# A cross-attention kernel: transposed context of the last two tiles from memory, weight scans spread over the tiles

## What is computed

```python
x1 = layernorm(x)                                # x2 = x1_2 = ctx_2048
energy = jnp.einsum('bcn,bmn->bcm', x1, x2)      # b=16, c=64, m=1601, n=1024
attn = jax.nn.softmax(energy, axis=-1)
attn = attn / (RENORM_EPS + attn.sum(axis=1, keepdims=True))
x_r = jnp.einsum('bcm,bmn->bcn', attn, x1_2)
t = x1 - (jnp.einsum('oc,bcn->bon', conv_w, x_r) + conv_b[None, :, None])
# batch norm over (b, n), relu, x = x + x1 + relu(...)
```

## Time and profile before

| | |
|---|---|
| median of 3 runs | 1379.93 us (1379.62 to 1380.21) |
| the profiled execution | 1379.24 us, span 1377.4 us |
| TensorE busy | 1334.1 us (97%) |
| VectorE busy | 878.7 us (64%) |
| ScalarE busy | 495.1 us (36%) |
| stage one ends (last `weigh_ctx`) | 484.8 us from the start |

### The profile page before, as it was taken

One profiled execution on the slowest core, in us unless ns is written; L12 is line 12 of the kernel. 1 busy time (PEld: TensorE's weight loads), 2 busy tenths in 40 slices (PEclk: granted clock), 3 DMA queues, 4 the chain that ended last, 5 costly groups with the idle time before them and its releaser, 6 DMA issues.

```text
span 1377.4 us, 17833 instructions
## 1 busy us (share of the span) xinstructions
PE 1334.1 (97%) x6850; PEld 651.2 (47%) x6850; DVE 878.7 (64%) x1484; ACT 495.1 (36%) x765; POOL 2.4 (0%) x10
## 2 busy tenths in 40 slices
PE   7999999999999979999999999999999999999994
PEld 4554646444454434444555555444444444444442
DVE  3232424324242288888889996755999997777974
ACT  1121302113021122116877775112545455544432
POOL 0000000000000000000000000000000000000000
PEclk9999999999999989999999999999999999999998
DMA  9999999999999587845565669341487775222264
GB/s 379 419 421 420 421 422 420 422 421 421 417 398 393 234 321 255 315 168 164 161 182 154 172 174 339 107 168 52 167 271 226 242 264 196 77 77 77 77 180 152
DMA packets 141044, 356.25 MB, mean 259 GB/s; under 512 B 63008, under 2 KB 89760, under 8 KB 115360
## 3 DMA queue, kind: packets, MB, share of 16 engines
q1 hardware_dynamic: 137792, 343.56, 68.5%
q10 hardware_dynamic: 3168, 11.54, 2.1%
HBM read 308.40 MB, written 46.66 MB: 258 GB/s over the span
## 4 chain that ended last, share of the span: by engine, by line
PE 74%; issue 14%; DMA 6%; DVE 4%; ACT 1%; DVEq 0%; POOLq 0%; POOL 0%
PE ps L1048 13%; PE ps L1153 13%; PE ps L1309 9%; PE ps L1220 8%; PE ps L962 7%; PE ps L1269 6%; PE ps L1107 5%; PE ps L1000 4%; DMA ctxT<-in_ctxT 3%; PE ps L979 2%; PE ps L1030 2%; PE ps L982 2%; DMA w_scan<-in_w2t 1%; PE ps L1173 1%; DMA x_t<-in_x 1%
## 5 line engine op out<-in xcount | busy, mean ns | idle before, releaser
L1358 PE MATMUL ps<-t_half,hl 128*128 128x512 f16 x896 | 193.6, 379 | 0.0
L1048 PE MATMUL ps<-ctx_sb,attnT 128*64 128x512 f32 (+1 forms) x832 | 180.3, 593 | 0.0
L699 ACT ACTIVATE stg<-ps 128x512 f32<-128x512 f32 (+1 forms) x80 | 44.4, 555 | 345.5 <-PE ps L979 173.4
L1358 PEld LDWEIGHTS ps<-t_half,hl 128*128 128x128 f16 x896 | 87.7, 98 | 105.7
L962 PE MATMUL ps<-ctxT,x1T 128*64 128x512 f32 x512 | 115.8, 596 | 1.8 <-DMA ctxT<-in_ctxT 1.8
L872 ACT ACTIVATE hl<-hb,al 128x512 f16<-128x512 f32 x112 | 79.2, 720 | 97.4 <-PE ps L1358 83.7
L1048 PEld LDWEIGHTS ps<-ctx_sb,attnT 128*64 128x64 f32 (+1 forms) x832 | 58.9, 137 | 115.4 <-issue 108.0
L1862 DVE SCALAR_TENSOR_TENSOR hl<-hb,al,hl 128x512 f16<-128x512 f32 x112 | 81.9, 749 | 48.7 <-ACT hl L872 48.5
L1107 PE MATMUL ps<-wv_sb,x2T 128*128 128x512 f32 x256 | 112.0, 596 | 0.0
L1220 PE MATMUL ps<-wo_sb,oT 128*128 128x512 f32 x256 | 111.6, 593 | 0.3 <-ACT oT L778 0.3
L1456 DVE COPY stg<-ps 128x512 f32<-128x512 f32 (+1 forms) x80 | 50.9, 639 | 82.2 <-PE ps L982 43.0
(11 more groups left out here) (220 smaller groups left out, 1810.5 us busy)
## 6 DMA issues: line engine op xcount, KB each, us to landing
ctxT<-in_ctxT SPq DMA_DIRECT2D x64, 1024.0 KB, 22.4
...
ctx_sb<-in_ctx SPq DMA_DIRECT2D x16, 2048.0 KB, 32.5
...
```

Of the source, the lines that this page charges most:

```text
L1048: ins = mm(bank(ea + hf)[C * b:C * b + C, :], attnT[0:w, slots[mt], C * b:C * b + C], ctx_sb[0:w, mt, b, hf * BANK:hf * BANK + BANK], star ...
L1358: ins = mm(bank(b), hl[:, r % RING, n, s * P:s * P + P], t_half[:, r % BRING, :], start=(fresh and k == 0 and n == 0), stop=(k == HK - 1 a ...
```

## The change

The host supplies two more arrays: `ctxW`, the transposed copy of the 512 wide rows (1 MB holds two of the 8 chunks), and `ctxE`, the transposed tail of the last tile (two parts of 0.27 MB). `LOADED` says how many of the eight wide chunks a tile takes from memory: none in tiles 0 to 5, four in tile 6, eight in tile 7, which also takes its tail from there. Tile 6 so has six pairs in place of ten, tile 7 none. Two of the 1 MB pieces go through the ring of `ctxT`, behind the tile's eight chunks; the other two of tile 7 go to `stg`, and its tail to the places of `x_t` and of a part of `x1T`, once tile 6's energies are done (`load_apart`). The last tile's groups of `ctx_sb` are loaded in the order in which `weigh_ctx` takes them. `tok` and `xo` are loaded in two parts each, and the second parts stand behind `wv_sb`. 40 scans in place of 48 stand in the value stage: 2 in tile 2, 6 in tile 3, 7 in each of tiles 4 to 7 and 4 behind, each tile's in three portions, one of them between the statistics and the square root's use. 24 in place of 16 stand in the projection stage, four ahead of `normal(H)` and four in each tile until they are done.

```diff
@@ -56,16 +56,40 @@
 U = len(UNITS)
 
 SINGLES = [(mt, half) for mt in range(TM, MT) for half in range(2)]
-PAIRS = [("wide", c) for c in range(NC)] + SINGLES[-2:]
-E = len(PAIRS)
-assert len(SINGLES) == E
+LOADED = (0,) * (NT - 2) + (4, NC)
+
+
+def pairs(p):
+
+    if p < BY_ROW:
+        return SINGLES
+    return [("wide", c) for c in range(LOADED[p], NC)] + (SINGLES[-2:] if p < NT - 1 else [])
+
+
+def first_pair(p):
+
+    return sum(len(pairs(q)) for q in range(p))
+
+
+def slots_of_tile(p):
+
+    ring = [(p, "chunk", c) for c in range(NC)] + [(p, "wide", i) for i in range(min(LOADED[p] // 2, 2))]
+    return ring if p < NT - 1 else ring + [(p, "apart", i) for i in range(2)]
+
+
+USES = [use for p in range(NT) for use in slots_of_tile(p)]
+USE_NO = {use: n for n, use in enumerate(USES)}
+RING_NO = {use: n for n, use in enumerate([use for use in USES if use[1] != "apart"])}
+RING_USES = list(RING_NO)
+
 H = 8
 D = 64
 HID = 4096
 HC = HID // P
 WT = HID * N // P // 1024
 WH = WT // H
-SCANS_V = 48
+SCANS_V = 40
+V_SCANS = (0, 0, 2, 6, 7, 7, 7, 7, 4)
 EPS = 1e-5
 LAMBDA_INIT = 0.8 - 0.6 * math.exp(-0.3 * 12)
...
@@ -382,6 +407,18 @@
 
         def width(mt):
             return P if mt < MT - 1 else TAIL
+
+        def slot(use):
+
+            return ctxT[:, RING_NO[use] % SLOTS, :, :] if use[1] != "apart" else stg[:, 2 * use[2]:2 * use[2] + 2, :, :]
+
+        def halves(use):
+
+            return slot(use) if use[1] == "apart" else slot(use).rearrange("p c (b m) -> p c b m", b=2)
+
+        def used_by(p):
+
+            return USE_NO[p, "chunk", NC - 1] + 1
...
-            def load_T(q, chunks):
+            def load_T(q, chunks, kind="chunk"):
                 for c in chunks:
-                    k = NC * q + c
+                    use = (q, kind, c)
+                    k = RING_NO[use]
                     if k >= SLOTS:
-                        sp.wait_ge(ctxT_used, k - SLOTS + 1)
-                    sp.dma_start(ctxT[:, k % SLOTS, :, :], ctxT_in[q, c]).then_inc(ctxT_got[k % SLOTS], 16)
+                        sp.wait_ge(ctxT_used, USE_NO[RING_USES[k - SLOTS]] + 1)
+                    to, src = (slot(use), ctxT_in[q, c]) if kind == "chunk" else (halves(use), ctxW_in[q, c])
+                    sp.dma_start(to, src).then_inc(ctxT_got[k % SLOTS], 16)
+
+            def load_apart():
+
+                sp.wait_ge(e_done, first_pair(NT - 1))
+                for i in range(2):
+                    sp.dma_start(slot((NT - 1, "apart", i)), ctxW_in[NT - 1, 2 + i]).then_inc(apart_got, 16)
+                for i in range(2):
+                    sp.dma_start(tails[i][:, :, :, :], ctxE_in[i]).then_inc(apart_got, 16)
...
                     load_T(p + 1, range(7, NC))
+                    load_T(p + 1, range(min(LOADED[p + 1] // 2, 2)), "wide")
+                    if p + 1 == NT - 1:
+                        load_apart()
+                        next_N((5, 7, 0, 1, 2, 6, 3, 4))
+                        break
                     next_N(range(0, 5))
                 if p == 0:
                     sp.dma_start(lam_sb[:, 0:4 * D], lambdas.partition_broadcast(P)).then_inc(lam_in, 16)
                 if p + 2 < NT:
-                    load_T(p + 2, range(0, 4 if p < 2 else 2))
+                    load_T(p + 2, range(0, 4 if p < 2 or LOADED[p + 1] else 2))
                 next_N(range(5, 6))
-                if p >= 2 and p + 2 < NT:
+                if p >= 2 and p + 2 < NT and not LOADED[p + 1]:
                     load_T(p + 2, range(2, 4))
                 next_N(range(6, G))
                 if p + 2 < NT:
                     load_T(p + 2, range(4, 6))
 
...
-            sp.wait_ge(ctxT_used, NC * NT)
+            def load_tok(t0, t1):
+                sp.dma_start(tok[:, t0:t1, :], n_dram[t0:t1].rearrange("t p n -> p t n")).then_inc(n_in, 16)
+
+            def load_xo(t0, t1, s):
+                sp.dma_start(xo[:, t0:t1, :], x_v[t0:t1].rearrange("t p n -> p t n")).then_inc(s, 16)
+
+            sp.wait_ge(ctxT_used, len(USES))
             sp.wait_ge(n_stored, 16 * (NT - 1))
-            sp.dma_start(tok[:, 0:NT - 1, :], n_dram[0:NT - 1].rearrange("t p n -> p t n")).then_inc(n_in, 16)
+            load_tok(0, 2)
             sp.wait_ge(pv_done, G * NT - 7)
-            for i in range(2):
-                h4 = slice(4 * i, 4 * i + 4)
-                sp.dma_start(xo[:, h4, :], x_v[h4].rearrange("t p n -> p t n")).then_inc(s_in[i], 16)
+            load_xo(0, 2, s_in[0])
             sp.wait_ge(pv_done, G * NT - 3)
             sp.dma_start(wv_sb[:, :, :], wv.rearrange("(c p) n -> p c n", p=P)).then_inc(wv_in, 16)
+            load_tok(2, NT - 1)
+            load_xo(2, NT, s_in[1])
             sp.wait_ge(pv_done, G * NT)
...
                     A(stg[:, e % 4, 0, 0:n], bank(pair_bank(p, e, 0), n), ACT.Copy).then_inc(act_tr_out, 1)
-                    if e == 2 and p + 1 < NT:
+                    if e == (2 if not LOADED[p] else 0) and p + 1 < NT:
                         sqrt(p + 2, slice(0, 1))
...
-                if t + 2 < NT:
+                if 1 <= t < NT - 2:
                     relu(t + 2)
...
                       ACT.Copy).then_inc(x2_out, 1)
+                if t == 0:
+                    act.wait_ge(n_in, 32)
+                    relu(2)
                 act.wait_ge(xs_ready, t + 1)
...
-                for g in [e // 2] if e % 2 == 0 and (p < BY_ROW or e == 8) else range(4) if e == 0 else []:
+                for g in [e // 2] if e % 2 == 0 and p < BY_ROW else range(4) if e == 0 else [4] if e == len(pairs(p)) - 2 else []:
...
+            def loaded_energies(p):
+
+                wides = [u for u in slots_of_tile(p) if u[1] != "chunk"]
+                for j, use in enumerate(wides):
+                    if use[1] == "apart":
+                        pe.wait_ge(apart_got, 64)
+                    else:
+                        k = RING_NO[use]
+                        pe.wait_ge(ctxT_got[k % SLOTS], 16 * (k // SLOTS) + 16)
+                    for i in range(2):
+                        c = 2 * j + i
+                        for b in range(2):
+                            ins = mm(bank(2)[C * b:C * b + C, :], x1T[:, p % 2, c, C * b:C * b + C], halves(use)[:, i, b, :],
+                                     start=(c == 0), stop=(c == NC - 1))
+                    ins.then_inc(ctxT_used, 1)
+
+            def tail_energies(p):
+                for c in range(NC):
+                    for b in range(2):
+                        ins = mm(bank(3, TAIL)[C * b:C * b + C, :], x1T[:, p % 2, c, C * b:C * b + C],
+                                 tails[c // 4][:, c % 4, b, :], start=(c == 0), stop=(c == NC - 1))
+                ins.then_inc(e_done, 1)
...
-                if p + 1 < NT:
+                if p + 1 < NT and LOADED[p + 1]:
+                    chunk_energies(p + 1, range(4, NC))
+                    if p == 5:
+                        loaded_energies(6)
+                        two(pair_transposes, 6, 0)
+                        two(pair_transposes, 6, 2)
+                        two(pair_energies, 6, 0)
+                        later_pairs(6)
+                    else:
+                        loaded_energies(7)
+                        tail_energies(7)
+                elif p + 1 < NT:
...
-                if t % 4 == 0:
-                    V.wait_ge(s_in[t // 4], 16)
+                if t in (0, 2):
+                    V.wait_ge(s_in[t // 2], 16)
...
-                    if e == 7:
-                        V.wait_ge(ctxT_used, NC * (p + 1))
+                    if e == len(pairs(p)) - 3:
+                        V.wait_ge(ctxT_used, used_by(p))
                         own.done(V.tensor_reduce(mx4[:, 0:1], ps[:, ea * BANK:(ea + 2) * BANK], AX.X, ALU.max))
-                    if e == 5 and p + 1 < NT:
+                    if e == len(pairs(p)) - 5 and p + 1 < NT:
                         make_x1(p + 1)
-                V.wait_ge(e_done, E * p + E - 2)
+                if p < NT - 1:
+                    V.wait_ge(e_done, first_pair(p + 1) - 2)
+                else:
+                    V.wait_ge(ctxT_used, used_by(p))
+                    own.done(V.tensor_reduce(mx4[:, 0:1], ps[:, ea * BANK:(ea + 2) * BANK], AX.X, ALU.max))
+                    V.wait_ge(ctxT_used, len(USES))
                 own.done(V.tensor_reduce(mx4[:, 1:2], bank(2), AX.X, ALU.max))
                 if p + 1 < NT:
                     put_x1T(p + 1)
-                V.wait_ge(e_done, E * p + E)
+                V.wait_ge(e_done, first_pair(p + 1) if p < NT - 1 else first_pair(p) + 1)
                 own.done(V.tensor_reduce(mx4[:, 2:3], bank(3, TAIL), AX.X, ALU.max))
                 V.tensor_reduce(nmx[:, :], mx4[:, 0:3], AX.X, ALU.max, negate=True).then_inc(nmax_ready, 1)
...
-            def norm2(t):
...
+            def norm2(t, scans=0):
                 if t:
                     V.wait_ge(relu_done, t + 1)
```

(25 more changed lines are left out.)

49 lines of the change are left out of this document (31 added, 18 removed).

## The result

| | before | after |
|---|---|---|
| median | 1379.78 us (1377.90 to 1380.21, 4 runs) | 1365.80 us (1365.15 to 1366.60, 4 runs) |
| ratio | | 0.9902 (95%: 0.9884 to 0.9919) |
| profiled execution, span | 1379.24, 1377.4 us | 1365.15, 1363.3 us |

A forecast was written before the change was run, and what follows sets the result against it. TensorE was taken as the bound, with the DMA close behind. Tile 6's -3.6 and tile 7's -9.4 sum to -13.0 us, giving 1366.2 against the profiled execution and a median of 1366.9 us, range 1364.8 to 1371.5.

The forecast's parts named there:

- Tile 6: Stage one, tile 6: two transpose groups go -3.8, fewer product groups -0.4, wait for ScalarE's copy +0.6; -3.6 us in all.
- Tile 7: Stage one, tile 7: wide transposes -7.6, the tail's short ones -1.14, five product groups fewer -0.7; -9.4 us in all.
- TensorE's busy time: Whole kernel: TensorE's busy time should fall by about 13.6 us, its waits for DMA staying under 3 us.
- The loads: End of stage one: 6.5 pieces add 16.2 us of DMA; last `ctx_sb` lands at 463 to 466, 2 to 5 us early.
- The 358 GB/s of the Trainium skill: Loads up to the last `ctx_sb`: at this rate, 18 us more, TensorE waiting some 14, sum within 2 us of no change.
- the batch norm: Behind stage one: its gap is a chain of VectorE and stays as before.
- rival 1: Tile 7's `weigh_ctx` waits for late DMA, from about 5 us of lateness; chance 0.06 slower, 0.05 within 0.2% of before.
- The value stage: Value stage: VectorE waits 6 us for the first scan, periods stay 14.6 us; cost 0, at most 2 us.
- Rival 2: Value stage, tiles 4 to 7: VectorE late as scans wait for loads, 2 to 6 us, time 1369 to 1373; chance 0.12.
- `kT`: After the last value tile: fewer VectorE scans gain only TensorE's 0.3 us wait for `kT`, not counted in the sum.
- Rival 3: Tile 6 transposes or ring slots wait for each other; at most all tile 6's gain goes, 1370.5 us; chance 0.07.

## Why the prediction held, step by step

**Tile 6** (-3.6): -3.63 measured, with a wait of 0.57 for ScalarE where 0.6 was put. The run with the root behind the copies shows the cause.

**Tile 7** (-9.4): -9.49. The row of 32 products takes 7.04 + 3.60 + 3.60 us less the overlaps, the tail 1.10.

**TensorE's busy time** (-13.6): -12.6 over the span. In tiles 6 and 7 it fell by 4.20 (3.63 and the wait of 0.57) and 9.49, 13.7 together. The difference lies before tile 6, where both kernels have the same instructions for TensorE: there it was busy for 360.8 us against 359.8. In tile 0 it waited 0.86 us for a load in place of 0.42, and the same products behind took longer, in a stretch (17 to 27 us) with a granted clock of 0.83 against 1.00. Before and after:

```profile
21.03 1.97 PE L1000 MATMUL ps<-stg,x1T 128*64 128x128 f32 x32
```
```profile
22.37 2.98 PE L1061 MATMUL ps<-stg,x1T 128*64 128x128 f32 x32
```

Against that its waits for loads were smaller before tile 6, 1.3 us against 2.9. The prediction counted only the 1.8 us for `ctxT`; another 1.1 were for `ctx_sb`, in three places.

**The loads.** The rate held: 406 to 430 GB/s in every 4 us from 400 to 464, and the gap at 408 is filled. What the prediction did not say is that the queue would run dry at 368 to 380 us: SyncE issued nothing from 358 to 373.48, since the four chunks of tile 7 that now stand ahead of tile 6's 4 MB group wait for slots. Against 420 GB/s that is 2.5 us of loads (an estimate from the three stretches), and everything behind lands that much later. The last load of `ctx_sb` was to land at 463 to 466 and be wanted at 468.3. With two pieces more it landed at 469.35; 2 MiB at 424 GB/s are 4.9 us, so it lands at 464.4 in the changed kernel, and is wanted at 448.80 + 19.96 = 468.8. The slack was 4.4 us, forecast 2 to 5. The 358 GB/s of the Trainium skill ("DMA: Bandwidth & Descriptors", section "Where 436 GB/s comes from") did not bind: every 4 us from 400 to 464 show over 400 GB/s. The kernel runs on one core alone; no run shows the rate with a second one.

**What the prediction did not see** is that these loads were not the thinnest place. It counted the landing of `xo` for the scans' sake and took the batch norm as a chain of VectorE that "stays". VectorE's first use of `xo` stands ahead of that chain, and there is no slack there, where `ctx_sb` has 4.4 us. Whether it can be had back, by putting that scaling behind the batch norm or by a smaller first load, was not tried. The chance of 0.06 + 0.05 for late loads was therefore put on the wrong place: rival 1 did not need 5 us of lateness to begin; any lateness would do. By that, an estimate, a rate 1% lower over the 107 us of loads would have cost 1 us. That the forecast was not hurt by it is partly luck: the load of `xo` came within 0.1 us of being in time.

**The value stage** (0, at most 2): +0.16 from its start to the first head, and the periods are 14.61 us. VectorE waited 7.05 us for the first scan (forecast 6). The lead of 4.3 us was that of the last tile but one; it is 2.7 now, and that of the last tile shrank from 3.4 us to 1.2. Rival 2 was nearly there: with the same numbers of scans in one portion the tiles are late from tile 5 on. The argument against it, that three portions let the four buffers be refilled, is what the run without portions shows. Its price was too low: 2 to 6 us forecast, 11 measured where the portions are taken away, since it counted VectorE's lateness and not the slower work behind each wait.

**`kT`**, not counted, came as a gain of 0.3. **Rival 3** did not occur. The forecast of 1366.9 was 1.1 us above the result. By the trace that is 0.5 us ahead of tile 6, which is scatter between executions and no merit of the change, 0.3 for `kT`, and a few tenths at the end of the kernel; the terms for tiles 6 and 7 were right to 0.1 us each.
